# Block scores on 64 rows, experts' first product by Strassen, and all orders of a two-layer kernel laid anew

## The reference, cut to what matters

```python
# layer 0: attention inside blocks of 64 tokens, 16 heads of 16
attn = softmax(einsum('bhnld,bhnmd->bhnlm', qb, kb))        # sc0, wt0
out = einsum('bhnlm,bhnmd->bhnld', attn, vb)                 # tp0, pv0, out0
# layer 0: coupling network, 3 cycles                        # gc, cn1..cn4, gate0, fin0
# layer 1: 8 heads of 64, 512 x 512 causal scores
term1 = where(causal, 0, qc_s @ vu.T)                        # term
look  = where(causal, sigmoid(qu_s @ ku.T), 0)               # look
scores = qc_s @ kc.T - silu(term1 @ look.T)                  # sc, su, sw
out = softmax(scores) @ vc                                   # turn, attend, out1
# layer 1: expert choice, 8 experts, 128 tokens each per batch
g, m = top_k(probs, 128); xin = x[m]                         # pos, index, fetch, turn_x
h = gelu(einsum('nekd,edf->nekf', xin, w1))                  # hidden (seven in the change); d 256, f 1024
h = einsum('nekf,efd->nekd', h, w2)                          # output
out = zeros.at[m].add(g * h)                                 # scatter
```

## Time and profile before

| | us |
|---|---|
| median of 3 runs | 1942.31 |
| lowest, highest run | 1942.08, 1942.38 |
| the profiled execution's span | 1941.7 |
| PE busy in it | 1911.9 |
| DVE busy | 1093.9 |
| ACT busy | 919.0 |
| POOL busy | 694.8 |

### The profile page before, as it was taken

One profiled execution on the slowest core, in us unless ns is written; L12 is line 12 of the kernel. 1 busy time (PEld: TensorE's weight loads), 2 busy tenths in 40 slices (PEclk: granted clock), 3 DMA queues, 4 the chain that ended last, 5 costly groups with the idle time before them and its releaser, 6 DMA issues.

```text
span 1941.7 us, 30308 instructions
## 1 busy us (share of the span) xinstructions
PE 1911.9 (98%) x11192; PEld 1317.8 (68%) x11192; DVE 1093.9 (56%) x2904; ACT 919.0 (47%) x1970; POOL 694.8 (36%) x769
## 2 busy tenths in 40 slices
PE   8989999999999999999999999999999999999998
PEld 5835655765575666557656655665786888888887
DVE  5767676558556746656585655577534447223221
ACT  5646666556565555655665566454334321111111
POOL 3302334334332433252343324343443433333332
PEclk9989999999999999999999999999999999999999
DMA  3020001000000100010001000050130223333333
GB/s 129 2 87 15 12 1 39 1 23 12 28 23 1 39 1 23 1 39 15 9 13 28 13 10 15 23 176 2 31 85 4 59 73 98 66 76 79 85 76 70
DMA packets 59696, 76.78 MB, mean 40 GB/s; under 512 B 7120, under 2 KB 52824, under 8 KB 59296
## 3 DMA queue, kind: packets, MB, share of 16 engines
q1 hardware_dynamic: 46448, 57.28, 8.9%
q0 software_dynamic: 12288, 16.79, 5.0%
q10 hardware_dynamic: 816, 0.79, 0.1%
HBM read 53.71 MB, written 21.00 MB: 38 GB/s over the span
## 4 chain that ended last, share of the span: by engine, by line
PE 96%; DVE 2%; ACT 1%; DMA 0%; issue 0%; POOL 0%; SPq 0%; ACTq 0%; DVEq 0%; POOLq 0%
PE bank L765 15%; PE bank L982 12%; PE bank L995 11%; PE bank L832 7%; PE bank L887 4%; PE bank L856 4%; PE bank L868 4%; PE bank L781 3%; PE bank L750 3%; PE bank L591 3%; PE bank L900 3%; PE bank L617 3%; PE bank L841 3%; PE bank L712 2%; PE bank L818 2%; PE bank L692 2%
## 5 line engine op out<-in xcount | busy, mean ns | idle before, releaser
L1232 ACT ACTIVATE h<-bank 128x512 f32<-128x512 f32 x128 | 76.3, 597 | 363.9 <-PE bank L982 352.8
L982 PE MATMUL bank<-xin,ew 128*128 128x256 f32 x1024 | 234.3, 381 | 0.0
L995 PE MATMUL bank<-ew,h 128*128 128x256 f32 x1024 | 226.7, 379 | 0.0
L1776 POOL TENSOR_TENSOR s<-s,ri 128x256 f32<-128x256 f32 (+3 forms) x128 | 160.0, 1268 | 156.5 <-DVE ri L1531 156.5
L995 PEld LDWEIGHTS bank<-ew,h 128*128 128x128 f32 x1024 | 194.2, 190 | 27.7 <-issue 1.5
L982 PEld LDWEIGHTS bank<-xin,ew 128*128 128x128 f32 x1024 | 189.5, 190 | 23.4 <-issue 0.2
L1814 POOL DMA_INDIRECT out<-y,indices x64 | 104.2, 1628 | 265.9 <-DVE y L1668 164.9
L1208 ACT ACTIVATE s<-s,mn 128x128 f32<-128x128 f32 (+3 forms) x256 | 141.0, 552 | 109.0 <-DVE mn L1524 108.9
L1509 DVE SCALAR_TENSOR_TENSOR th<-th,bank 128x384 f32<-128x384 f32 (+1 forms) x192 | 104.3, 594 | 112.0 <-ACT th L1199 110.6
L1668 DVE SCALAR_TENSOR_TENSOR y<-bank,gates,gbe 128x256 f32<-128x256 f32 x64 | 31.0, 484 | 238.5 <-PE bank L995 230.1
L832 PE MATMUL bank<-look,term 128*128 128x384 f32 (+3 forms) x512 | 152.7, 438 | 0.0
(11 more groups left out here) (320 smaller groups left out, 3641.3 us busy)
## 6 DMA issues: line engine op xcount, KB each, us to landing
ew<-L_ffn_w SPq DMA_DIRECT2D x24, 1024.0 KB
x1s<-x_scratch SPq DMA_DIRECT2D x8, 512.0 KB
out<-x1s SPq DMA_DIRECT2D x8, 512.0 KB, 2.9
xn_scratch<-n_xn SPq DMA_DIRECT2D x8, 512.0 KB, 2.9
x<-L_attn_x SPq DMA_DIRECT2D x7, 512.0 KB, 3.8
x_scratch<-x SPq DMA_DIRECT2D x7, 512.0 KB, 3.0
wqkv<-w_qkv SPq DMA_DIRECT2D x1, 3072.0 KB, 10.7
wqkv<-L_wmod SPq DMA_DIRECT2D x2, 1024.0 KB, 8.0
```

The costliest lines, as they stand in the source:

```text
L982: mm = te.matmul(banks[i][:, g * 2 * P:(g + 1) * 2 * P], w1[:, kk, (2 * n + g) * P:(2 * n + g + 1) * P], xin[:, kk, :, :].rearrange("p h s ...
L995: mm = te.matmul(banks[i][:, 0:D], ex.h1[:, g, n * P:(n + 1) * P], w2[:, g, :], start=(g == 0), stop=(g == FC - 1))
L1776: done = g.tensor_tensor(sc, sc, b1.ri[u % 2][:, m, :].unsqueeze(2).to_broadcast([P, 2, w]), ALU.mult)
```

## The change

- An sc0 step does two blocks (4 steps a batch). The contraction runs over 64 rows: upper and lower rows take turns, each into a bank of its own, with 128 columns a matmul. k's buffer is half as large and is written by two ACT activations over all rows, with masks by strip (`row`, `bkr`); it needs no zeros, and clearing it is dropped. DVE's and ACT's steps handle two blocks at once; POOL weights with two instructions and signals once.
- Units 0 to 27 make their first product in seven steps (n = 0 to 3; 1, 2, 3 and 1 products) instead of hidden: seven products of half the size, each 4 matmuls of 128 columns. Four go into one bank (`i1`) upon each other; between them ACT copies (`first_read`) or DVE adds (`chain_read`) what stands there. POOL forms sums of the weights (`mix_w`, 4 additions a load), DVE sums of the inputs (`mix_x`, 4 a unit). Units 28 to 31 are unchanged. NBUF is 2.
- HEAD, PERIOD and LAST are written anew. In HEAD, `1x0` comes before `0x0`; `1rows` and `1cols` come earlier, `1twist` later.

```diff
-NBUF = 3
+NBUF = 2
+def seven(m):
+    return m < NUNIT and UNITS[m][2] < E
...
+    if seven(m):
+        yield "seven", m, 0
+        if m + 3 < NUNIT:
+            yield "pick", m + 3, 0
+        yield "seven", m, 1
+        yield "seven", m, 2
+        if m + 1 < NUNIT:
+            yield "turn_x", m + 1, 0
+        yield "seven", m, 3
...
 # tensor_engine, sc0
-            for c in range(KC):
-                mm = te.matmul(banks[i][:, c * 256:(c + 1) * 256], f.q[:, c, n, :, :].rearrange("p a l -> p (a l)"),
-                               f.k[:, c, n, :, :].rearrange("p r m -> p (r m)"), start=True, stop=True)
-            mm.then_inc(full[i], 1)
+            for blk in range(2):
+                for c in range(KC):
+                    for h, rows in enumerate(HALVES):
+                        i, nth = at[step, b, n, h]
+                        out = banks[i][:, :].rearrange("p (b r c m) -> p b r c m", b=2, r=2, c=KC)
+                        mm = te.matmul(out[:, blk, :, c, :],
+                                       f.q[rows, c, 2 * n + blk, :, :].rearrange("p a l -> p (a l)"),
+                                       f.k[rows, c, 2 * n + blk, :, :], start=True, stop=True)
...
 # tensor_engine, experts
+            def product(bank, left, right):
+                for g in range(FC // 2):
+                    mm = te.matmul(banks[bank][:, g * P:(g + 1) * P], left[:, g * P:(g + 1) * P], right,
+                                   start=True, stop=True)
+            def chained(left, right, first):
+                for g in range(FC // 2):
+                    mm = te.matmul(banks[i1][:, g * P:(g + 1) * P], left[:, g * P:(g + 1) * P], right,
+                                   start=first and g == 0, stop=True, skip_group_check=True)
+            if n == 0:
...
+                chained(w1[:, 0, 0:F // 2], xin[:, 0, 0, :], True).then_inc(s["chain"], 1)
+            elif n == 1:
+                te.wait_ge(s["mixed_w"], 4 * (load + 1))
+                te.wait_ge(s["mixed_x"], 4 * (b + 1))
...
+                product(i5, sums[:, 0, :], xt[:, 0, :]).then_inc(full[i5], 1)
+                te.wait_ge(s["first_read"], b + 1)
+                chained(sums[:, 1, :], xt[:, 1, :], False).then_inc(s["chain"], 1)
+            elif n == 2:
...
+                product(i3, sums[:, 2, :], xin[:, 1, 1, :]).then_inc(full[i3], 1)
+                te.wait_ge(s["chain_read"], 2 * b + 1)
+                chained(w1[:, 0, F // 2:F], xt[:, 2, :], False).then_inc(s["chain"], 1)
...
+                product(i2, w1[:, 1, 0:F // 2], xin[:, 1, 0, :]).then_inc(full[i2], 1)
+            else:
+                te.wait_ge(s["chain_read"], 2 * b + 2)
+                chained(w1[:, 1, F // 2:F], xt[:, 3, :], False).then_inc(full[i1], 1)
...
 # scalar_engine, seven
+            if n == 0:
+                a.wait_ge(s["chain"], 3 * b + 1)
+                a.copy(ex.h1[:, tops, 0:P], banks[i1][:, :].rearrange("p (f s) -> p f s", f=FC // 2)).then_inc(s["first_read"], 1)
...
 # vector_engine, seven
+            if n == 1:
+                v.wait_ge(s["chain"], 3 * b + 2)
+                v.wait_ge(drained[i5], n5)
+                v.tensor_tensor(ex.h1[:, tops, P:2 * P], chain, ex.h1[:, lows, P:2 * P], ALU.add
+                                ).then_inc(s["chain_read"], 1)
+            elif n == 2:
...
+                v.wait_ge(s["chain"], 3 * b + 3)
+                v.tensor_tensor(ex.h1[:, lows, P:2 * P], chain, ex.h1[:, lows, P:2 * P], ALU.add
+                                ).then_inc(s["chain_read"], 1)
...
+            elif n == 3 and seven(b + 1):
+                v.wait_ge(full[i1], n1)
+                mix_x(b + 1)
...
 HEAD = """
-    0stats:0 0silu:0 1stats:0 0wqkv_load:0 0mod_load:0 0x0:0 0norm:0 1norm:0 0cols:0 0setup:0 1x0:0 0mod_load:1
...
+    0mod_load:0 0stats:0 0silu:0 1x0:0 1stats:0 0cols:0 0norm:0 1norm:0 0wqkv_load:0 0cols:1 0feat:0 1feat:0 0x0:0
...
```

More of the change, by code:

```diff
@@ L77 @@
+    0sc:11 0attend:9 0turn:10
 """
 PERIOD = """
[L82 to L95, removed]
+    proj:0.3 proj:0.1 +stats:0 proj:0.2 +feat:0 +norm:0 proj:0.0 +kq:0 +kq:1 -weigh:11 -x1_load:0 +v:1 term:0 look:0.0
@@ new lines @@
+    +sc0:0 look:0.1 +sc0:1 +wt0:0 +wt0:1 -attend:10 +v:0 look:0.2 proj:1.0 proj:1.3 +tp0:1 proj:0.4 +ga0_load:0
+    turn_vu:0 +tp0:0 -turn:11 +tp0:3 +tp0:2 +pv0:0 w:0.0 -o_out:3 w:0.1 -attend:11 +pv0:1 su:0 sw:0 +sc0:2 sc:0 +wt0:2
+    +sc0:3 weigh:0 -out1:0 +x0:0 vc:0 -out1:1 proj:1.1 proj:1.2 +tp0:4 +wt0:3 +tp0:5 -stats_t:0 turn_vu:1 proj:1.4
+    +tp0:6 turn:0 +bias0:0 +pv0:2 -norm_t:0 +tp0:7 su:1 look:1.0 sw:1 su:2 sw:2 w:1.0 +pv0:3 term:1 look:1.1 sc:1 sc:2
+    weigh:1 +out0:0 vc:2 vc:3 +out0:1 vc:1 -feat_t:0 weigh:2 su:3 -gate:0 su:4 +stats:1 sw:3 attend:0 sw:4 +norm:1
@@ new lines @@
+    look:1.2 turn:1 proj:2.2 proj:2.1 -softmax:0 +feat:1 sc:3 sc:4 attend:1 turn:2 proj:2.0 w:1.1 +cn1:0 +gc:0 look:2.0
+    +cn2:0 turn_vu:2 +gc:1 attend:2 o_out:0 +cn3:0 w:2.0 +gc:2 weigh:3 look:2.1 +cn4:0 +twist:0 proj:2.4 su:5 +cn1:1
+    weigh:4 sw:5 +cn2:1 look:2.2 +cn3:1 proj:2.3 turn:3 sc:5 term:2 +cn4:1 proj:3.2 proj:3.1 w:2.1 +cn1:2 su:7 su:6
+    attend:3 sw:6 sw:7 +cn2:2 turn_vu:3 turn:4 +cn3:2 weigh:5 sc:6 attend:4 weigh:6 proj:3.0 turn:5 +cn4:2 proj:3.3 su:8
+    sw:8 attend:5 o_out:1 look:3.0 +gate0:0 turn:6 look:3.1 sc:7 sc:8 weigh:7 term:3 look:3.2 +fin0:0 weigh:8 w:3.0
@@ L190, with half_of, new_load @@
 LAST_OF = [max(m for m in range(NUNIT) if UNITS[m][2] == n) for n in range(E + FIRST)]
-NBUF = 3
+NBUF = 2
 FIRST_LATE = min(m for m in range(NUNIT) if UNITS[m][1] == NQ - 1)
+def seven(m):
+    return m < NUNIT and UNITS[m][2] < E
+def half_of(m, n):
+    return 1 - n if seven(m) else n
+def new_load(m):
+    return seven(m) and UNITS[m][2] != UNITS[m - 1][2]
 def experts_steps(m):
@@ L253, in products @@
         return KC if n == 0 else 0
+    if step == "seven":
+        return SEVEN[n]
     return PRODUCTS.get(step, 0)
@@ L1086, in scalar_engine @@
         elif step == "sc0":
-            i, nth = at[step, b, n, 0]
-            a.wait_ge(drained[i], nth)
-            a.activation(f.s[n % 2][:, :, :, :], f.s[n % 2][:, :, :, :], ACT.Exp).then_inc(f.sem["exp0"], 1)
+            for h in range(2):
+                i, nth = at[step, b, n, h]
+                a.wait_ge(drained[i], nth)
+            a.activation(f.s[n % 2][:, :, :, :, :], f.s[n % 2][:, :, :, :, :], ACT.Exp).then_inc(f.sem["exp0"], 1)
         elif step == "tp0":
@@ L1806, in pool_engine @@
         elif step == "output":
[L1807 removed]
+            q, half = UNITS[b][1], half_of(b, n)
             w = 2 * b + n
```

357 lines of the change are left out of this document (222 added, 135 removed).

## The result

The changed kernel takes 1955.34 us (median of 4 runs, 1952.89 to 1955.98) against 1942.19 for the kernel before (also 4 runs): a ratio of 1.0067, interval 1.0053 to 1.0081, so it is slower by 13 us, clear of noise though under 1%. That lies inside the range of 1932 to 1957, but not at the 1944 of the likeliest case; it is the case that had 0.34. The profiled execution spans 1951.6 us, 9.9 more than that of before; a second profile of the same kernel (e1) spans 1955.5.

What follows compares the result with a forecast made beforehand. PE was taken to bound the kernel, busy 1911.9 of 1941.7 us. Queue -12.0, chained bank +7.5 and +1.0, head +3.8, stalls elsewhere +1.0 gave +1.3 on 1942.3: 1943.6, said as 1944, range 1932 to 1957.

Steps and rivals of the forecast that it cites:

- the likeliest case: The whole kernel with all terms as priced: +1.3 us, 1944 us (1939 to 1946.2), chance 0.35.
- The queue's prices: PE's queue: block scores -26.8, seven products -18.6, shape changes +33.4, together -12.0 us.
- part 2: First products of 28 units, seven products for eight: 56 records at 0.1115 us a unit, -18.6 us.
- Part 3: PE's tile shape: 178 more changes, each 0.094 us on leaving and 0.05 to 0.10 on entering, +33.4 us.
- The ordinary pause of the chained bank: Between a unit's products: second 0.07 late, third 0.17, made 0.3 us a unit; 25 units, +7.5 us.
- the "+1" of part 4: Chained bank's readers standing behind other instructions in 9 units among attention steps: +1 us (0 to 8).
- The +1 for stalls elsewhere: Outside the head: stalls from laying 619 shape changes and their readers anew, +1 us (-1 to +4).
- The start: Head, x1s loaded first: PE starts 3.3 us later, less some 0.5 that kq waits less, +2.8 us.
- the head would waste 1.0 of its gain: Part of HEAD's -4.0 us falls where PE waits for DVE and ACT anyway: +1.0 us (0 to +4).
- The slower one: Chained bank's readers queue on ACT or DVE behind attention's instructions: +8 us, about 1952 us, chance 0.34.
- The faster one: 128-column records at 0.109 us, first hand-over hidden, HEAD keeps its gain: -7.7 us, about 1936 us, chance 0.28.
- Loads that set the pace, and halves that run one after the other: Seven products paced by 0.19 us loads: 2046 us; 64-row score products not side by side: 1971 us; chance 0.03 together.

Runs made afterwards that it cites:

- e1: The changed kernel run once more, unchanged: 1955.70 us.
- e5: The kernel before with only neighbouring steps of different batches exchanged, so that the array's shape changes 591 times instead of 441: 1982.91 us.
- e3: The changed kernel with units 9 to 15 making hidden steps again instead of Strassen's seven steps: 1949.25 us.
- e10: The kernel before with Strassen's steps in 17 late units, choosing steps spread three to a unit, none beside GpSimd's sums: 1935.29 us.
- e7: The kernel before with Strassen's steps in 18 late units and choosing steps spread, four to a unit: 1942.65 us.
- e8: The changed kernel with choosing steps spread four to a unit, five late loads instead of four, and 0x0 loaded first: 1952.37 us.
- e2: The changed kernel with only HEAD's load 0x0 put back ahead of 1x0: 1953.65 us.
- e6: The changed kernel with steps of different batches moved by up to two places, for 558 shape changes instead of 619: 1997.10 us.
- e12: e9 and e10 in one kernel, with the first transpose of a batch's block scores moved later: 1934.56 us, ratio 0.9960 to the kernel before.
- e9: The kernel before's orders with the changed kernel's two-block, 64-row sc0 steps and no Strassen: 1960.55 us.
- e4: The kernel before, its own orders kept, with Strassen's steps in units 9 to 27 alone and two weight buffers: 1956.58 us.

## Why the prediction was right and wrong

**The queue's prices were right.** 32 sc0 steps of 0.89, 56 records at 0.1115 to a unit's first product, and 0.09 and 0.05 to 0.10 for a change of shape gave -12.0; the trace gives -12.3. In the changed kernel a sc0 step behind an sw step and ahead of an sc step, entered and left without a change, shows its bare price:

```profile
536.54 1.06 PE L657 MATMUL bank<-k0a,q0a 64*128 64x128 f32 x16
537.43 0.82 PE L898 MATMUL bank<-kc,qc 64*128 64x128 f32 x8
```

537.43 - 536.54 = 0.89. For the 0.1115, part 2 says that the trace of before has no record of 128 columns behind a full load but in transposes. It has: each su step of full shape starts with such records (L832, 128x128), and their median spacing there is 0.111 us, which would have settled 0.1115 against 0.109 beforehand.

Part 3, the term that ate the gain of the scores, is what e5 confirmed: 3.50 us for 18 changes. The Trainium skill's sentence on the tiling mode (TensorEngine Tiling (Array Packing), Key Properties), which names a drain and no price, agrees with it; of the two, the price is what the sum needed.

**The ordinary pause of the chained bank was right.** A unit among the late ones:

```profile
1791.90 1.10 PE L1042 MATMUL bank<-xint,ew1s 128*128 128x128 f32 x8
...
1792.84 1.06 PE L1036 MATMUL bank<-xin,ew1s 128*128 128x128 f32 x8
1793.04 0.69 DVE L1794 TENSOR_TENSOR h<-bank,h 128x512 f32<-128x512 f32 x1 [0.56 <-PE bank L1042]
...
1793.78 0.97 PEld L1042 LDWEIGHTS bank<-xint,ew 128*128 128x128 f32 x8
...
1794.78 1.06 PE L1036 MATMUL bank<-xin,ew 128*128 128x128 f32 x8
...
1795.67 0.60 PE L1009 MATMUL bank<-ident,xrows 128*128 128x128 f32 x4
```

The product of 1791.90 takes 0.94 to the next (0.05 above its 0.89), that of 1793.78 1.00, and the steps n = 1 and 2 are 0.05 and 0.16 longer than their products; I had 0.07 and 0.17. With a repeating unit of 14.09 us against 14.54, Strassen brings 0.45 a unit, not the 0.37 of my terms: the pauses are 0.21 us a unit and not 0.3. Rounding up to 0.3 was the only thing wrong there.

**The step that failed is the "+1" of part 4.** I named the mechanism, readers that queue, and the point at which it decides, a reader more than 0.1 us late. But I looked for it among attention's steps and priced it at 1, with 8 for the rival. There, ahead of 1590 us, PE's idle time for the chained bank's readers is 0.2 us in all. It sat in units 9 to 12, beside the sixteen choosing steps of 1.44 us on DVE: +10.8 us. Their places could be read from the list (two choosing steps between seven 1 and seven 2 of unit 9), and before the change they cost nothing, because only work with slack stood behind them (PE is 100.00 us busy of 100 from 1600 on): a change that gives an engine a deadline makes old work on its queue expensive. e3 (the work of the units put back) and, in the old order, e10 (the choosing steps moved away) show it from opposite sides. e7 and e8 show that choosing steps are not the whole of it: DVE's queue there was also lengthened by its additions beside GpSimd's sums. In the changed kernel's own order only e8's spread was run, which freed nothing; that e10's would is not shown.

**Where else.** The +1 for stalls elsewhere was 5.4, spread over some fifteen places between 250 and 1350 us, of which no experiment took one by itself. The start was right in size (3.4 for 3.3) and worth about 2 in the end by the medians of runs that overlap (e2), where I had 2.8; that the head would waste 1.0 of its gain was wrong in sign, it waited 2.1 less in the profile, though 0.6 more in the second one. The two large misses, +9.8 and +4.4, are both waits, and the other experts' steps gave 3.0 back; the range held because the rival's price was in it.

**The rivals.** The slower one was right in kind and in size (1952), wrong in place, so that its size came near is luck: its 8 us were nine units among attention's steps at 0.3 a hand-over, and what came was 10.8 in four units behind them and 5.4 that isn't the chained bank's. The faster one's 0.109 is out: the products run at 0.892 / 8 = 0.1115. Loads that set the pace, and halves that run one after the other, are out by the same rows; so is, for this form, the ratio of 81 to 56 from the Trainium skill (TensorE: Matmul & The Clock Gate, Back-to-back issue gap). Its price was also miscounted in the prediction: 56 records at 0.156 instead of 0.1115 us are 2.5 us a unit and 70 us for 28, where 52 is the distance to the kernel before. And the range's lower end, the faster rival with no hand-over charged, would by its own terms have been 1930, not 1932; neither bears on the result.

## What to carry to other kernels

When a change makes PE wait for a reader inside a chain, walk that reader's queue over the whole program and price whatever stands ahead of it, the old work above all; it costs nothing today only because nobody waits behind it. A saving on PE's queue that comes with a new order has to be counted with the changes of tile shape (here 0.2 us each, 178 of them against 45 us of gain), and then the order has to be checked reader by reader: moving steps by one or two places brought some 50 us of waiting (e6). Take the two halves of such a change apart, keep the old order, and repair the few waits that the profile names; that gained 7 us (e10, e12) where the whole lost 13.

## What the runs showed of the hardware that I hadn't expected

- A pause can be dearer than itself, but not each one is. After 2.97 us of waiting at 363.56 us (e9) PE took 0.88 us for four transposes of 0.44 and 2.79 for a projection of 1.81; after 9.57 us (e4) 1.86 and 1.71 for two products of 0.89. These records run at half pace, which is the lower level, 1.2 GHz; the granted clock of e9's stretch from 358 to 366 us is 0.81. Yet the same 2.97 us in e9's next three PERIODs are followed by full pace (granted clock 1.00 from 542 to 546 us). So are the changed kernel's 1.93 us at 1635.03, while its 1.83 us at 1619.46 aren't, and in e1 the same wait of 1.83 us is followed by full pace. In the kept traces, behind 154 us, PE ran at the lower level after all seven pauses of more than 3.5 us, and after 8 of the 25 of 1.8 to 3.0 us. A pause in this second group can't be given one price.
- DVE's additions of two SBUF operands (128x128) took 0.28 us alone; beside GpSimd's additions of 128x512 (about 1.3 us each) three of the four in e7's rows took 1.31 to 1.81, about as long as one of GpSimd's or more. The Trainium skill (SBUF — State Buffer, SBUF: two separate sides) calls the port that these two share an exclusive lock held for a whole instruction; the rows of e7 agree. DVE's additions with one operand in PSUM (0.67 to 0.69 us) and its MAX8 (0.68 to 0.69) last the same beside GpSimd's sums in the changed kernel.
- 128 columns behind a full weight load of 0.19 us pass at 0.1115 us a record, the pace of the gate in the earlier trace rows, although a load as recorded is longer.
